# A decoder on one core: spread keys written by four GpSimd instructions, attention values copied by ScalarE

## The chip, the core and the metric

The kernel runs on one core of a Trainium2 chip. The core has five engines that run their own instruction queues and meet only at semaphores: TensorE (PE, matmuls, and PEld for its weight loads), VectorE (DVE), ScalarE (ACT), GpSimd (POOL) and SyncE (SP, here only DMA issues). They share the on-chip memory SBUF; TensorE writes its results to PSUM, which VectorE and ScalarE read. The metric is the time of one execution of the whole program in microseconds of the device.

## What is computed

The reference is a decoder of four layers with twelve steps on a hidden state of 64 x 64 x 128 floats (64 sequences of 64 tokens, width 128), each step added to the state. Three of its six attentions have 16 heads of width 8 over the tokens of one sequence, and keys of their own; two take keys and values from a second input, the context. The change touches the attentions of layers 1 to 3. Cut to what matters (`_layernorm` is a plain normalisation):

```
def _L1_attn_ref(x, Wqkv, bqkv, Wout, bout):              # phase a1
    q, k, v = split(x @ Wqkv + bqkv)                      # 16 heads of 8
    attn = softmax(q k^T / sqrt(8)); return (attn v) @ Wout + bout

def _L2_xattn_ref(query, key, value, wq, bq, wk, bk, wv, bv, wo, bo):   # phase x2
    q, k, v = query wq^T + bq, key wk^T + bk, value wv^T + bv
    attn = softmax(q k^T / sqrt(8)); return (attn v) wo^T + bo

def _L3_attn_ref(x, Wq, bq, Wk, bk, Wv, bv, Wo, bo, gamma, beta, rel_bias):  # phase a3
    xn = layernorm(x) * gamma + beta
    attn = q k^T * scale + rel; masked causally; softmax
    return (attn v) @ Wo.T + bo                           # v = xn @ Wv.T + bv

def _L3_xattn_ref(query, key, value, wq, wk, wv, bq, bk, bv):           # phase x3
    q, k, v = grouped_linear(...)                         # each with its bias
    src_max = maximum(max(score), 0)
    attn = exp(score - src_max) / (sum + exp(-src_max))   # restricted softmax
    return attn v                                         # no output projection
...
x = x + _L3_attn_ref(_layernorm(x), ...)
x = x + _L3_xattn_ref(_layernorm(x), ctx_1024, ctx_1024, ...)
```

## The kernel before

The program is a row of twelve phases, each closed by a barrier of all engines: a0, w0, f0, a1, x1, f1, a2, x2, f2, a3, x3, f3. The state `k.x` stays in SBUF all the time as 32 tiles of 128 tokens (two sequences each); eight groups of four tiles (`NG` = 8, `GT` = 4) go through each phase.

Function `attention` (L263) writes five of them: a0, a1, x2, a3 and x3. It writes one queue for each engine by hand, as Python loops over the 32 tiles i, with g the group and t = 0 to 3 the tile in it. Nothing is reordered later: the order of an engine is the order of these lines, and semaphores are the only ties between engines.

For each tile: TensorE `score(i+1)` (L847) makes scores of all 16 heads in one PSUM tile `S` of 128x1024; it works with *spread keys* `kbd`, in which each head has its own copy of the keys, multiplied by a mask `mask8` that keeps the 8 rows of that head. VectorE adds the relative bias where there is one (`add_bias`, L553, a3 only), takes the highest (L560, or L636 in a3), in x3 raises it to zero (a tensor_scalar, L647), and subtracts it into `e` (`shift`, L563). ScalarE takes the exponential in two halves (`exps`, L733). TensorE turns `e` into `TP` (`turn`, L858), ScalarE copies `TP` into `pT` in two halves (L738), TensorE weighs the values `vx` with it into `AV` (`weigh`, L871), and VectorE divides by the sums (`take_sums` and `take_values`, L534 and L548). All are staggered: while tile i is turned and weighed, tile i+1 is shifted and made exponential, and VectorE takes the values of tile i-1.

Between those steps, once in a group, stand the steps `early(g, t)` and `late(g, t)` of each engine:

- Values: `take_v(n, other)` of VectorE (L488 on) brings the projected values, from `PJ` (PSUM) or for kv="ctx" from `vin` (SBUF), into `vx`, where each head pair of the two sequences has its place. It is four instructions of 64x256 (L494), which also add the bias row `vb`; two stand before `shift` of t = 0 and two behind it. `v_ready` releases `weigh` and, in a1 and a3, the use of `PJ` by `turn_att` (L825) at t = 1.
- Keys: ScalarE writes heads 4 to 7 of `kbd` (`spread_keys`, L716, one instruction each: two at t = 0, one at t = 1, one at t = 2), GpSimd writes heads 0 to 3 (`spread_half`, L401) in one instruction of 128x2048. GpSimd waits for the keys (`kT_ready`, L708, at t = 3 for the group after the next, or the load of the context's keys) and for the last scores that read this half of `kbd`.
- Layernorm: VectorE takes statistics (t = 1) and gathers them (t = 2), GpSimd raises them to -0.5 (`norm_root`, L393), VectorE makes `nmr` from mean and root (`shift_mean`, L468, a scalar_tensor_tensor of 128x4, at t = 3), ScalarE normalises (L679, two tiles at t = 0 and two at t = 1), TensorE turns (L798, t = 2).
- Output: TensorE turns the attention output (L825) and projects it (L831), VectorE adds it to the state (`update`, L526), and GpSimd has by then added the output bias `ob` to the state (`bias_x`, L408). In x3 there is no output projection: `update` is L521, at t = 0.

The order of GpSimd in the loop is `bias_x(g)`, `norm_root(g + 3)`, `spread_half(g + 2)`. In the startup VectorE runs `whole_norm` of groups 0 and 1, then `take_v(0)`, in a3 the bias table `bt`, then `whole_norm(2)`; ScalarE works off groups 0 and 1, in a3 with a copy of the table's first product between them (`u`, L775), which TensorE multiplies (L918) before it turns group 1.

Function `warping` (L944, phase w0) also projects the context for the later phases, into DRAM: `project_memory` (L1255 on) and `stage_memory`, five products for each group, named in `jobs`. They run while VectorE works through a chain of small steps.

## Time and profile before

| what | us |
| --- | --- |
| median of 3 runs | 2355.95 (2353.13 to 2364.38) |
| the profiled execution, its own time | 2360.56 |
| its span in the trace | 2358.8 |
| phase a1 (L263 with tag a1), from its first to its last work | 707 to 889 |
| phase x2 | 1428 to 1593 |
| phase a3 | 1671 to 1885 |
| phase x3 | 1885 to 2065 |

Over the span TensorE is busy 76%, VectorE 57%, ScalarE 47%, GpSimd 31%; but phases differ, so each is read alone. The views used below are the timeline (instructions of one engine in order of time: start in us, duration in us, engine, line, operation, tile written and tiles read, shapes, count where several in a row are merged, and in brackets the idle time ahead of it and who ended it), the groups of instructions of a stretch (line, engine, operation, shapes, count, then busy us and mean ns of one, then idle time ahead and its releasers), and the windows (length of the stretch, busy us of PE, PEld, DVE, ACT and POOL with their counts, the granted clock of TensorE as a share of full speed, DMA share and GB/s). Durations of merged rows overlap by their tails: two copies of 0.58 follow each other at a distance of 0.49 and read 1.07 together.

### The profile page before, as it was taken

How to read it: one execution, taken by the hardware profiler on the slowest of the kernel's cores; microseconds unless marked ns; L12 is line 12 of the kernel's file. 1: busy time of each engine (PE TensorE's matmuls, PEld its weight loads, DVE VectorE, ACT ScalarE, POOL GpSimd, SP SyncE). 2: the span in 40 equal slices, each digit the busy share in tenths (PEclk: the TensorE clock that was granted, in tenths of full speed). 3: DMA queues.
4: the chain of work that ended last, by engine and by line, in shares of the span. 5: the costliest groups of instructions: out<-in, count | busy, mean ns of one | idle time of the engine just before them, and what ended most of it. 6: DMA issues, size and time to landing. Idle time of an engine off the chain costs nothing. (4 is left out here: it accounts for less than half of the span.)

```text
span 2358.8 us, 39307 instructions
## 1 busy us (share of the span) xinstructions
PE 1786.9 (76%) x14513; PEld 1229.5 (52%) x14513; DVE 1350.3 (57%) x3525; ACT 1103.6 (47%) x2265; POOL 730.6 (31%) x617
## 2 busy tenths in 40 slices
PE   3887562899987986778994886888788778851994
PEld 1554441545544664555994553655455535551774
DVE  2888578512235764554343467974399789851223
ACT  3676440333345766633442345763366566610441
POOL 1223201270463221155453003221222132156453
PEclk9888785699997998879997787999798878855997
DMA  4111272136615001112674001000000010012224
GB/s 152 82 83 83 86 246 58 28 98 165 177 48 213 33 2 55 29 38 99 213 236 154 1 1 36 29 10 10 3 2 2 2 45 24 6 40 69 64 80 137
DMA packets 143729, 173.18 MB, mean 73 GB/s; under 512 B 20913, under 2 KB 118897, under 8 KB 142609
## 3 DMA queue, kind: packets, MB, share of 16 engines
q1 hardware_dynamic: 123956, 129.09, 17.4%
q0 software_dynamic: 13248, 28.21, 3.5%
q10 hardware_dynamic: 6336, 13.37, 1.5%
q8 instruction: 118, 1.93, 0.3%
q14 instruction: 71, 0.58, 0.1%
HBM read 126.84 MB, written 79.05 MB: 87 GB/s over the span
## 5 line engine op out<-in xcount | busy, mean ns | idle before, releaser
L2770 POOL DMA_INDIRECT f_back<-f_ys,f_row x158 | 151.2, 957 | 173.7 <-DVE f_ys L2931 144.4
L871 PE MATMUL a_AV<-a_vx,a_pT 128*64 128x18 f32 (+1 forms) x3072 | 115.0, 223 | 42.3 <-DVE a_att L548 16.3
L2763 POOL DMA_INDIRECT f_slots<-f_pay,f_slot x128 | 124.5, 972 | 66.0 <-issue 38.2
L871 PEld LDWEIGHTS a_AV<-a_vx,a_pT 128*64 128x64 f32 x3072 | 105.9, 146 | 71.1 <-issue 36.7
L733 ACT ACTIVATE a_e<-a_e 128x512 f32<-128x512 f32 x192 | 110.2, 622 | 67.6 <-DVE a_e L563 67.6
L858 PE MATMUL a_TP<-ident,a_e 128*128 128x128 f32 x768 | 110.2, 288 | 19.0 <-ACT a_e L733 18.4
L738 ACT COPY a_pT<-a_TP 128x512 f32<-128x512 f32 x192 | 103.7, 588 | 41.9 <-PE a_TP L858 41.7
L858 PEld LDWEIGHTS a_TP<-ident,a_e 128*128 128x128 f32 x768 | 91.4, 148 | 57.5 <-ACT a_e L733 45.8
L847 PE MATMUL a_S<-a_kbd,a_qT 64*64 64x512 f32 x768 | 118.3, 693 | 0.9 <-issue 0.6
L563 DVE TENSOR_TENSOR a_e<-a_S,a_mx 128x1024 f32<-128x1024 f32 x96 | 117.3, 1221 | 2.9
L560 DVE TENSOR_REDUCE a_mx<-a_S 128x16 f32<-128x1024 f32 x66 | 80.8, 1224 | 42.8 <-PE a_S L847 41.6
L2997 ACT ACTIVATE f_h<-f_H,f_wt 128x256 f32<-128x256 f32 x156 | 67.0, 474 | 81.5 <-PE f_H L3093 81.5
L2997 ACT ACTIVATE f_h<-f_H,f_b 128x512 f32<-128x512 f32 (+1 forms) x96 | 57.7, 616 | 83.3 <-PE f_H L3093 83.3
L858 PEld LDWEIGHTS x_TP<-ident,x_e 128*128 128x128 f32 x512 | 62.5, 153 | 61.3 <-ACT x_e L733 51.7
L871 PE MATMUL x_AV<-x_vx,x_pT 128*64 128x18 f32 x2048 | 77.1, 219 | 21.8 <-ACT x_pT L738 15.0
L858 PE MATMUL x_TP<-ident,x_e 128*128 128x128 f32 x512 | 78.6, 300 | 17.8 <-ACT x_e L733 17.5
L560 DVE TENSOR_REDUCE x_mx<-x_S 128x16 f32<-128x1024 f32 x64 | 78.1, 1220 | 22.5 <-PE x_S L847 22.1
L871 PEld LDWEIGHTS x_AV<-x_vx,x_pT 128*64 128x64 f32 x2048 | 71.9, 148 | 35.4 <-issue 25.7
L1653 ACT ACTIVATE f_h<-f_H,f_b 128x512 f32<-128x512 f32 x64 | 44.0, 687 | 94.0 <-PE f_H L1761 93.9
L393 POOL TENSOR_TENSOR a_rstd<-a_var,neghalf 128x4 f32<-128x4 f32 x24 | 24.3, 1015 | 204.9 <-DVE a_var L464 120.9
L716 ACT ACTIVATE a_kbd<-a_kT,a_mask 128x512 f32<-128x512 f32 x128 | 85.6, 723 | 0.4
L401 POOL TENSOR_TENSOR a_kbd<-a_kT,a_mask 128x2048 f32<-128x2048 f32 x16 | 57.6, 3600 | 85.8 <-ACT a_kT L708 85.8
(481 smaller groups left out, 4611.8 us busy)
## 6 DMA issues: line engine op xcount, KB each, us to landing
f_wt<-in_f_ew SPq DMA_DIRECT2D x39, 584.0 KB
f_slots<-in_blank SPq DMA_DIRECT2D x1, 18576.0 KB
f_wt<-in_f_leaf SPq DMA_DIRECT2D x94, 98.0 KB, 2.0
f_pay<-f_back SPq DMA_DIRECT2D x8, 1024.0 KB, 5.6
f_xs<-f_slots SPq DMA_DIRECT2D x47, 144.0 KB
memory_x_k<-w_stage ACTq DMA_DIRECT2D x24, 256.0 KB, 3.1
f_slots<-in_blank SPq DMA_DIRECT2D x1, 5760.0 KB
f_xs<-leaf_slots SPq DMA_DIRECT2D x22, 256.0 KB, 3.6
```

What stands on the lines that cost most here:

```text
L401: pool.tensor_tensor(kbd[:, n % 2, :, 0:4, :], bc(keys(n).rearrange("p (b j) -> p b j", j=SL), 2, shape), mask8[:, 0:4].unsqueeze(1).unsqu ...
L560: return v.tensor_reduce(mx[:, i % 2, :], unit(i), AX.X, ALU.max)
L563: v.tensor_tensor(e[:, i % 2, :, :], unit(i), bc(mx[:, i % 2, :], 2, [P, NH, SL]), ALU.subtract).then_inc(shifted.sem, 1)
L716: last = act.activation(kbd[:, n % 2, :, h, :], keys(n).rearrange("p (b j) -> p b j", j=SL), ACT.Copy, scale=mask8[:, h:h + 1])
L733: act.activation(eh, eh, ACT.Exp).then_inc(weights.sem, 1)
L738: act.copy(pT[:, 4 * n:4 * n + 4, :], TP[:, n, :].rearrange("p (a b) -> p a b", a=4)).then_inc(pT_half.sem, 1)
L847: last = pe.matmul(S[64 * c:64 * c + 64, i % 2, r, :], qT[rows, g % 2, SL * b:SL * b + SL], kbd[rows, g % 2, b, :, :], start=True, stop=True)
L858: last = pe.transpose(TP[:, half, P * n:P * n + P], ev[:, 4 * half + n, :], k.ident[:, :])
L871: last = pe.matmul(AV[64 * c:64 * c + 64, 2 * hp * W1:2 * (hp + 1) * W1], pT[:, hp, 64 * c:64 * c + 64], vx[:, g % 2, t, c, 2 * hp:2 * hp ...
L2763: pool.indirect_dma_start(out=slots[:, :], out_offset=bass.IndirectOffsetOnAxis(ap=slot[:, c, t:t + 1], axis=0), in_=pay[:, c, t, :], in_o ...
L2770: pool.indirect_dma_start(out=back[:, :], out_offset=bass.IndirectOffsetOnAxis(ap=row[:, i % RR, t:t + 1], axis=0), in_=ys[:, i % RY, t, : ...
L2997: act.activation(h[:, i % 2, c, 0:P * n], hid(i, c, n), ACT.Gelu_apprx_tanh, bias=weights(i)[2][:, c:c + 1])\
```

## The change

Four things change.

1. `spread_half` writes heads 0 to 3 in four GpSimd instructions, each for two of the eight sequences of the group (128x512), in a1, x2, a3 and x3. The semaphore is raised by the last one.
2. In a3 and x3 (`act_moves=True`) VectorE no longer has `take_v`; ScalarE does it, as four copies of 64x256 without bias, behind the two copies of `pT` at t = 0, and for group 0 in the startup. Of the keys, ScalarE then spreads head 4 at t = 0, heads 5 and 6 at t = 1 and head 7 at t = 2.
3. The values' bias of a3 goes to the output: since the weights of a row sum to one, bias times output matrix is added to the output bias once, by one TensorE product at the start of the phase and one VectorE add into `obr`, which `bias_x` then adds.
4. The values' bias of x3 goes into the context's projection in w0: four further products with one row each (a column of ones times the bias row), for each group.

```
@@ spread_half
-                    shape = [P, 2 * GT, 4, SL]
-                    pool.tensor_tensor(kbd[:, n % 2, :, 0:4, :], bc(keys(n).rearrange("p (b j) -> p b j", j=SL), 2, shape),
-                                       mask8[:, 0:4].unsqueeze(1).unsqueeze(3).to_broadcast(shape), ALU.mult).then_inc(kbd_pool.sem, 1)
+                    shape = [P, 2, 4, SL]
+                    kv = keys(n).rearrange("p (b j) -> p b j", j=SL)
+                    for b in range(0, 2 * GT, 2):
+                        last = pool.tensor_tensor(kbd[:, n % 2, b:b + 2, 0:4, :], bc(kv[:, b:b + 2, :], 2, shape),
+                                                  mask8[:, 0:4].unsqueeze(1).unsqueeze(3).to_broadcast(shape), ALU.mult)
+                    last.then_inc(kbd_pool.sem, 1)
@@ bias_x
+                    if g == 0 and obr is not None:
+                        pool.wait_ge(ob_ready.sem, 1)
+                    added = obr[:, :] if obr is not None else k.row(ob)
@@ VectorE: early, late
-                    if g + 1 < NG:
+                    if g + 1 < NG and not act_moves:
                         take_v(g + 1, False)
...
@@ VectorE: startup
+            if not act_moves:
+                v.wait_ge(setup_done.sem, 2)
+                take_v(0, False)
+                take_v(0, True)
+            elif obr is not None:
+                v.wait_ge(ob_product.sem, 1)
+                v.tensor_tensor(obr[:, :], AV[:, 0:P], k.row(ob), ALU.add).then_inc(ob_ready.sem, 1)
@@ ScalarE
+            def take_v(n):
+                if cross:
+                    act.wait_ge(kv_in[n % 2].sem, kv_in[n % 2].after(n // 2))
+                else:
+                    act.wait_ge(v_product.sem, v_product.after(n))
+                if n >= 2:
+                    act.wait_ge(values.sem, values.after(GT * (n - 2) + GT - 1))
+                for half in range(2):
+                    for seq in range(2):
...
+                        last = act.copy(vx[rows, n % 2, :, seq, half:NH:2, 0:width], src)
+                last.then_inc(v_ready.sem, 1)
             def late(g, t):
+                if act_moves and t == 0 and g + 1 < NG:
+                    take_v(g + 1)
                 if t < 3 and g and g + 1 < NG:
-                    spread_keys(g + 1, ((0, 1, 2), (3, 4, 5), (6, 7))[t] if diff else ((4, 5), (6,), (7,))[t])
+                    spread_keys(g + 1, ((0, 1, 2), (3, 4, 5), (6, 7))[t] if diff else
+                                ((4,), (5, 6), (7,))[t] if act_moves else ((4, 5), (6,), (7,))[t])
@@ ScalarE: startup, behind spread_keys(0) and take_q(0)
+            if act_moves:
+                act.wait_ge(setup_done.sem, 2)
+                take_v(0)
@@ TensorE
+            if obr is not None:
+                pe.matmul(AV[:, 0:P], k.col(vb).to_broadcast([P, P]), k.mat(o), start=True, stop=True).then_inc(ob_product.sem, 1)
@@ project_memory in w0
+                            if bias is not None:
+                                last = pe.matmul(banks[n][:, tok], ones[0:1, 0:1].to_broadcast([1, P]), k.row(bias)[0:1, :], start=False, stop=True)
```

How the queues stand before and after at the places that matter. First ScalarE in a3, in the first group that spreads keys, from the last tile of the group before to the second tile of this one, before:

```order
L738 COPY a_pT<-a_TP 128x512 x2
L716 ACTIVATE a_kbd<-a_kT,a_mask 128x8x64 x2
L679 ACTIVATE a_xn<-x,a_nmr,a_rstd 128x128 x2
L733 ACTIVATE a_e<-a_e 128x512 x2
L679 ACTIVATE a_xn<-x,a_nmr,a_rstd 128x128 x2
L725 COPY a_attT<-a_PJ 128x512
L738 COPY a_pT<-a_TP 128x512 x2
L716 ACTIVATE a_kbd<-a_kT,a_mask 128x8x64
L733 ACTIVATE a_e<-a_e 128x512 x2
```

The same stretch after:

```order
L768 COPY a_pT<-a_TP 128x512 x2
L747 COPY a_vx<-a_PJ 64x4x8x8 x4
L729 ACTIVATE a_kbd<-a_kT,a_mask 128x8x64
L692 ACTIVATE a_xn<-x,a_nmr,a_rstd 128x128 x2
L763 ACTIVATE a_e<-a_e 128x512 x2
L692 ACTIVATE a_xn<-x,a_nmr,a_rstd 128x128 x2
L755 COPY a_attT<-a_PJ 128x512
L768 COPY a_pT<-a_TP 128x512 x2
L729 ACTIVATE a_kbd<-a_kT,a_mask 128x8x64 x2
L763 ACTIVATE a_e<-a_e 128x512 x2
```

Four copies now stand ahead of the exponentials of the second tile, one spread of keys has moved behind them. In x3 it is the same without `a_attT`.

Then ScalarE in the startup of a3, where `a_u` is the first product of the bias table, before:

```order
L708 ACTIVATE a_kT<-a_PJ,cols 128x512
L716 ACTIVATE a_kbd<-a_kT,a_mask 128x8x64 x4
L775 COPY a_u<-a_S 32x1024
L687 ACTIVATE a_xT<-a_PJ,cols 128x512
L697 ACTIVATE a_qT<-a_PJ,cols 128x512
```

and after:

```order
L721 ACTIVATE a_kT<-a_PJ,cols 128x512
L729 ACTIVATE a_kbd<-a_kT,a_mask 128x8x64 x4
L747 COPY a_vx<-a_PJ 64x4x8x8 x4
L811 COPY a_u<-a_S 32x1024
L700 ACTIVATE a_xT<-a_PJ,cols 128x512
L710 ACTIVATE a_qT<-a_PJ,cols 128x512
```

The copies of the values stand between the keys and the copy that the bias table waits for.

## Rows read from the trace of the kernel before

**Rows 1.** Windows: one of a1, one of a3, two of x3.
```profile
780.00:800.00 20.00, 18.34 (x225) 12.12 (x224) 15.63 (x34) 15.47 (x31) 5.86 (x3) 1.00 0.01 2
...
1722.00:1845.00 123.00, 104.12 (x1160) 70.46 (x1161) 116.90 (x175) 80.88 (x148) 31.38 (x16) 0.89 0.01 2
...
1926.00:1946.00 20.00, 15.76 (x218) 9.96 (x216) 19.21 (x41) 15.51 (x33) 4.88 (x3) 1.00 0.09 27
...
1966.00:1986.00 20.00, 17.44 (x173) 11.52 (x171) 16.94 (x39) 12.69 (x27) 3.27 (x3) 0.66 0.01 2
```

**Rows 2.** Timeline of a3 from 1748 us: GpSimd, then VectorE.
```profile
1748.90 3.60 POOL L401 TENSOR_TENSOR a_kbd<-a_kT,a_mask 128x2048 f32<-128x2048 f32 x1 [2.57 <-ACT a_kT L708]
1752.46 1.27 POOL L408 TENSOR_TENSOR x<-x,rows 128x512 f32<-128x512 f32 x1
...
1749.01 3.51 DVE L468 SCALAR_TENSOR_TENSOR a_nmr<-a_mv,a_rstd 128x4 f32<-128x4 f32 x1
```

**Rows 3.** Timeline of x3 from 1944 us: GpSimd, then VectorE.
```profile
1944.30 3.60 POOL L401 TENSOR_TENSOR x_kbd<-x_kT,x_mask 128x2048 f32<-128x2048 f32 x1
...
1945.10 2.83 DVE L647 TENSOR_SCALAR x_mx<-x_mx 128x16 f32<-128x16 f32 x1
```

**Rows 4.** Two lines over the span: count, then ns minimum/median/maximum, first and last start.
```profile
L468 DVE SCALAR_TENSOR_TENSOR a_nmr<-a_mv,a_rstd x24: 149/161/3510, 28.8 to 1819.2; 128x4 f32<-128x4 f32 x24
...
L647 DVE TENSOR_SCALAR x_mx<-x_mx x30: 174/175/2836, 1916.1 to 2059.1; 128x16 f32<-128x16 f32 x30
```

**Rows 5.** Groups of instructions of a3, 1745 to 1843 us.
```profile
L733 ACT ACTIVATE a_e<-a_e 128x512 f32<-128x512 f32 x34 | 19.5, 622 | 18.0 <-DVE a_e L563 18.0
```

**Rows 6.** Groups of instructions of x3, 1926 to 2006 us.
```profile
L494 DVE TENSOR_TENSOR x_vx<-x_vin,rows 64x256 f32<-64x256 f32 x16 | 6.7, 418 | 0.2
```

**Rows 7.** Timeline of GpSimd: its spreads in a3 and x3, first and last of each.
```profile
1726.20 3.60 POOL L401 TENSOR_TENSOR a_kbd<-a_kT,a_mask 128x2048 f32<-128x2048 f32 x1 [2.56 <-ACT a_kT L708]
...
1842.87 3.60 POOL L401 TENSOR_TENSOR a_kbd<-a_kT,a_mask 128x2048 f32<-128x2048 f32 x1 [18.91 <-ACT a_kT L708]
...
1924.61 3.60 POOL L401 TENSOR_TENSOR x_kbd<-x_kT,x_mask 128x2048 f32<-128x2048 f32 x1
...
2005.00 3.60 POOL L401 TENSOR_TENSOR x_kbd<-x_kT,x_mask 128x2048 f32<-128x2048 f32 x1
```

**Rows 8.** Timeline of ScalarE in a3 from 1751 us: the start of a group.
```profile
1751.72 1.07 ACT L738 COPY a_pT<-a_TP 128x512 f32<-128x512 f32 x2 [1.45 <-PE a_TP L858]
1752.68 1.34 ACT L716 ACTIVATE a_kbd<-a_kT,a_mask 128x512 f32<-128x512 f32 x2
1753.91 0.87 ACT L679 ACTIVATE a_xn<-x,a_nmr,a_rstd 128x128 f32<-128x128 f32 x2
```

**Rows 9.** Timeline of the startups of x3 (VectorE, ScalarE) and x2 (VectorE).
```profile
1894.22 3.55 DVE L468 SCALAR_TENSOR_TENSOR x_nmr<-x_mv,x_rstd 128x4 f32<-128x4 f32 x1 [1.12 <-POOL x_rstd L393]
...
1897.81 1.65 ACT L679 ACTIVATE x_xn<-x,x_nmr,x_rstd 128x128 f32<-128x128 f32 x4 [2.04 <-DVE x_nmr L468]
...
1436.44 3.55 DVE L468 SCALAR_TENSOR_TENSOR x_nmr<-x_mv,x_rstd 128x4 f32<-128x4 f32 x1 [1.12 <-POOL x_rstd L393]
```

**Rows 10.** Timeline of VectorE inside x2, from 1502 us.
```profile
1502.13 1.34 DVE L468 SCALAR_TENSOR_TENSOR x_nmr<-x_mv,x_rstd 128x4 f32<-128x4 f32 x1
...
1504.20 1.23 DVE L560 TENSOR_REDUCE x_mx<-x_S 128x16 f32<-128x1024 f32 x1 [0.44 <-PE x_S L847]
```

**Rows 11.** Timeline of the startup of a3: ScalarE, then TensorE.
```profile
1689.54 1.00 ACT L775 COPY a_u<-a_S 32x1024 f32<-32x1024 f32 x1 [0.20 <-PE a_S L910]
...
1689.43 2.08 PE L815 MATMUL a_PJ<-mats,a_xT 128*128 128x128 f32 x8
1691.44 3.78 PE L918 MATMUL a_S<-a_u,a_mt 32*128 32x512 f32 x4
```

**Rows 12.** Timeline of TensorE in w0: its first work behind the context's projection.
```profile
386.76 0.64 PE L1286 MATMUL w_TX<-ident,w_C 64*64 64x32 f32 x8 [50.60 <-DVE w_found L1096]
```

**Rows 13.** Timeline of TensorE in x3: transposes behind a wait.
```profile
2040.97 1.97 PE L858 MATMUL x_TP<-ident,x_e 128*128 128x128 f32 x8 [1.24 <-ACT x_e L733]
```

More of the change, by code:

```diff
@@ L37 @@
 COLS = ["a0_g", "a0_b", "a1_bq", "a1_bk", "x1_nw", "a2_ga", "a2_be", "a2_bq", "x2_bq", "x2_bk",
-        "a3_bq", "a3_bk", "a3_ga", "a3_be", "x3_bq", "x3_bk"]
+        "a3_bq", "a3_bk", "a3_ga", "a3_be", "x3_bq", "x3_bk", "a1_bv", "x2_bv", "a3_bv"]
 ROWS = ["a1_bv", "a1_bo", "x1_gb", "x1_nw", "a2_bq", "a2_bk", "a2_bv", "a2_bqa", "a2_bka",
@@ L263, in attention @@
 def attention(nc, k, d, tag, q, kk, vv, o=None, kv="self", width=8, qb=None, kb=None, vb=None,
-              ob=None, affine=None, bias=False, restricted=False, diff=None, fill=None):
+              ob=None, affine=None, bias=False, restricted=False, diff=None, fill=None, act_moves=False):
     ph = Phase(nc, tag)
@@ L292, in attention @@
     attT = ph.sb("attT", [P, GT, P]) if o is not None else None
+    obr = ph.sb("obr", [P, P]) if act_moves and o is not None else None
+    ob_product, ob_ready = ph.counter("ob_product"), ph.counter("ob_ready")
     S = ph.ps("S", [P, 2, 2, 512])
@@ L407, in bias_x @@
                     pool.wait_ge(xn_ready.sem, xn_ready.after(g))
-                    pool.tensor_tensor(xg, xg, bc(k.row(ob), 1, [P, GT, P]), ALU.add).then_inc(x_biased.sem, 1)
+                    if g == 0 and obr is not None:
+                        pool.wait_ge(ob_ready.sem, 1)
+                    added = obr[:, :] if obr is not None else k.row(ob)
+                    pool.tensor_tensor(xg, xg, bc(added, 1, [P, GT, P]), ALU.add).then_inc(x_biased.sem, 1)
             def square(g):
@@ L595, in late @@
                 if t == 0:
-                    if g + 1 < NG:
+                    if g + 1 < NG and not act_moves:
                         take_v(g + 1, True)
@@ L718, in spread_keys @@
                     last.then_inc(kbd_ready.sem, 1)
+            def take_v(n):
[7 more added lines that the diff above has]
+                    for seq in range(2):
+                        src_rows, rows = slice(64 * seq, 64 * seq + 64), slice(64 * half, 64 * half + 64)
+                        src = flat(vin[src_rows, n % 2, :, :]) if cross else PJ[src_rows, :]
+                        src = src.rearrange("p (t h w) -> p t h w", t=GT, w=width)
+                        if not diff:
+                            src = src[:, :, half:NH:2, :]
+                        last = act.copy(vx[rows, n % 2, :, seq, half:NH:2, 0:width], src)
+                last.then_inc(v_ready.sem, 1)
             def take_att(g):
@@ L1187, in stage_memory @@
                     dst = stage[:, g % 2, n, :]
-                    if bias is None:
+                    if bias is None or not turned:
                         act.copy(dst, banks[n]).then_inc(staged.sem, 1)
@@ L1267, in project_memory @@
                             tok = slice(P * t, P * t + P)
-                            last = pe.matmul(banks[n][:, tok], cT[:, g % 2, tok], k.mat(name), start=True, stop=True)
+                            last = pe.matmul(banks[n][:, tok], cT[:, g % 2, tok], k.mat(name), start=True, stop=bias is None)
+                            if bias is not None:
+                                last = pe.matmul(banks[n][:, tok], ones[0:1, 0:1].to_broadcast([1, P]), k.row(bias)[0:1, :], start=False, stop=True)
                     last.then_inc(projected.sem, 1)
@@ L3201, in lay_out @@
             "x2_bq": i["L2_xattn_bq"], "x2_bk": i["L2_xattn_bk"], "a3_bq": i["L3_attn_bq"], "a3_bk": i["L3_attn_bk"],
-            "a3_ga": i["L3_attn_gamma"], "a3_be": i["L3_attn_beta"], "x3_bq": i["L3_xattn_bq"], "x3_bk": i["L3_xattn_bk"]}
+            "a3_ga": i["L3_attn_gamma"], "a3_be": i["L3_attn_beta"], "x3_bq": i["L3_xattn_bq"], "x3_bk": i["L3_xattn_bk"],
+            "a1_bv": bqkv[:, 2].reshape(P), "x2_bv": i["L2_xattn_bv"], "a3_bv": i["L3_attn_bv"]}
     d["cols"] = np.stack([cols[n] for n in COLS], axis=1)
```

11 lines of the change are left out of this document (4 added, 7 removed).

## The prediction

> **What bounds the kernel now.** Phases are closed by barriers, so what a phase gains comes off the total. I read the windows first [rows 1]. In a1 TensorE is busy 18.3 of 20 us and its clock is granted in full: matmuls and their hand-overs set the pace. In a3 VectorE is busy 116.9 of 123 us, in x3 19.2 of 20 where the clock is full. There it is VectorE, and ScalarE says the same: in a3 its exponentials waited 18.0 us in a stretch of 98, all for VectorE's subtraction [rows 5].
>
> Part of this busy time is no work. In a3 the tiny scalar_tensor_tensor L468 takes 3.51 us and ends at 1752.52, when GpSimd's spread that began 0.11 us before it ends at 1752.50 [rows 2]; its siblings take 0.15 [rows 4], and each of groups 0 to 4 of a3 has one like this. In x3 the tensor_scalar L647 takes 2.83 instead of 0.17 [rows 3, 4] and ends at 1947.93, the spread at 1947.90; it is 2.66 lost in each of the same groups. So these two kinds of VectorE instruction, all operands in SBUF, wait until a running GpSimd instruction ends. Reductions and subtractions from PSUM beside it keep their 1.2 us. And the hand-over happens between two GpSimd instructions that stand back to back: L408 starts at 1752.46 with nothing ahead of it missing, and L468 still ends at 1752.52 [rows 2].
>
> The pace is read off the spreads [rows 7]: six in a3 from 1726.20 to 1842.87, five steps, 23.3 us for a group; five in x3 from 1924.61 to 2005.00, four steps, 20.1 (three of 19.7, one of 21.3, the one whose window shows a clock of 0.66).
>
> **Part 1, four GpSimd instructions.** A piece costs between 0.90 (3.60 / 4) and 1.27, the price of another GpSimd tensor_tensor of 128x512, L408 [rows 2]. I take 1.0, between them and nearer the first, whose operands are these. The whole then ends 0.4 later (bounds 0 and 1.5); the keys are read a group later, `bias_x` behind it is read by `update` some five us later, so this is hidden; it would take over 4 us more to show. VectorE now waits for one piece at most. In a3 L468 comes 0.11 behind the start, so it waits about 0.9 instead of 3.36: 2.5 less, in five groups (0 to 4). In x3 the tensor_scalar falls late in the first piece and L468 behind it into the third: about 0.3 + 0.6 instead of 2.66, so 1.8 less, again in five groups and a bit in the sixth. In x2 one such wait is 1.34 long, but the reduction behind it then waits 0.44 for TensorE [rows 10], which had been busy: nothing is gained. In a1 the two do not meet. In the startups of x2 and x3 the L468 of group 1 is held for 3.55 and ScalarE waits for it 2.04 [rows 9]; without it ScalarE normalises earlier, then meets the query product that starts at the same time: I count 1.5 in x2 and 1.2 in x3 (bounds 0 and 2.0).
>
> **Part 2, the copies.** VectorE loses four instructions of 0.42 [rows 6], with their gaps 1.75 a group, seven times in each phase. ScalarE gains four copies that no row shows. From its pairs [rows 8] a spread of 512 elements takes 0.63 to the next, a normalisation of 128 takes 0.38, a plain copy of 512 takes 0.48: so 0.24 for 384 elements, and a plain copy of 256 would take 0.32. Bounds are 0.25 and 0.48. I take 0.33, 1.3 for four. The Trainium skill, Perfetto Trace Analysis, section Optimizing Scalar/DVE Operations, gives ScalarE about 51 ns of fixed cost on PSUM and 93 on SBUF, and advises larger operations on a saturated engine, which speaks against cutting work into four. Taking its 51 ns with the 1.2 GHz of the skill's first page, an estimate is 0.26 a copy, 1.1 for four, and the sum would gain about 3 us more; no row here shows it.
>
> **Is ScalarE then in the way?** At t = 0 it had 1.34 + 0.87 of spreads and normalisations ahead of the exponentials [rows 8], about 2.0 by distances; now 1.3 + 0.63 + 0.77 = 2.7, and 0.63 more at t = 1. Per group VectorE alone would need 23.3 - 1.75 - 2.5 = 19.1 in a3 and 19.7 - 1.75 - 1.8 = 16.2 in x3. I followed one group through the three queues, with what the timeline of these stretches gives as distances at full clock: scores 1.0, bias 1.1, highest 1.25, subtract 1.15 (a3 3.7 from scores to ready), half an exponential 0.6, transposes 1.0, copy 0.7, weighing 1.05, projections 1.0 each. In a3 the scores of successive tiles start at 0, 4.4, 11.0, 15.1, 20.1; in x3 at 0, 3.4, 9.0, 13.0, 17.4. The long second step is that of ScalarE: the copies delay the second tile's exponentials, and TensorE waits about 1.2 (a3) and 1.5 (x3) for them. So the pace becomes 20.1 in a3 and 17.4 in x3, 1.0 and 1.2 above VectorE's own.
>
> **Startup of a3.** Here the copies cost. The value product starts at 1689.43 and takes 2.08, the table's copy was done by 1690.54 and TensorE multiplied it from 1691.44 [rows 11]. Now ScalarE waits for the product (1691.5), copies values (1692.8) and the table (1693.9), and TensorE, which turns group 1 only behind that product, is 2.5 late.
>
> **Parts 3 and 4.** One product and one add of 128x128 in a3's startup stand where both engines idle: nothing. The 32 products in w0 follow work after which TensorE idles 50.6 us [rows 12]; each could take 1.5 before anyone waited. Nothing.
>
> **The sum.** a3: five steps of 3.2 = 16.0; first and last groups 1.0; startup -2.5; together 14.5. x3: four steps of 2.7 = 10.8; behind 2005.00 one wait of each kind and two value copies, 2.7 + 2.3 + 3.5 less 1.5 left over, of which half, since TensorE sets the end there: 3.5; the first group 1.5; startup 1.2; together 17. x2: 1.5. Total 33. The profiled execution took 2360.56, so 2327.6; the runs' median stands 0.2% under that, 2355.95, and 33 from it gives 2323. I take **2324**.
>
> **Rivals.**
>
> *TensorE's clock decides (more ScalarE than counted).* Copies at their bound of 0.48 add 0.6 a group. TensorE's waits then pass 1.8, and in x3 a wait of 1.24 was once followed by 1.97 for eight transposes [rows 13], twice the 1.0 above: the level of 1.2 GHz. Such a stretch costs 1.6 of a group now (21.3 against 19.7), with VectorE holding the pace; if it comes in half the groups at 2 us, 12 of the 33 go. With the copies 18 or so go: 2339. For it: more rests on TensorE now. Against it: a1 keeps the full clock with waits under 1 us.
>
> *No hand-over between pieces.* VectorE waits for all four, 0.4 longer than now. Then a3 goes at 21.9 and x3 at 18.4, 1.4 and 1.3 a group for seven groups, less 2.5: 2356 - 17 = 2340. The hand-over of [rows 2] speaks against it. The skill's page SBUF — State Buffer, section Who interferes with whom, has the shared port pair locked for a whole instruction, whoever comes first; by it the trace agrees with one piece of waiting, and it does not say who is served between pieces.
>
> *VectorE's bound alone.* If the copies hide (0.25 each), a3 runs at 19.2 and x3 at 16.3: 1 us more for 12 groups, 2311.
>
> *Slower: half clock all through.* If TensorE waits over 2 us behind the copies in each group, it may stay at 1.2 GHz for most of it. In x3 its 13.7 us of a group [rows 1] double to 27, in a3 17 to 34. It decides once half clock holds for over a quarter of a3's group (3.2 us lost) and a fifth of x3's. At 40% of each, a group of a3 takes 25 and one of x3 22: 2356 + 8 + 9 = 2373. The mean 0.89 in both phases [rows 1], with waits of 2.1, says that this is far.
>
> *Nothing shows.* If x3 and a3 were bound by TensorE anyway, 2355; the 18.0 us of ScalarE waiting for VectorE [rows 5] speak against it.
>
> **How the numbers follow.** Forecast 0.60 (2314 to 2333), clock 0.16, no hand-over 0.06, VectorE's bound 0.11, slower 0.04, nothing 0.03. A measurement of this kernel can tell 0.5%, about 12 us, from no change. Faster needs under 2344: the forecast, its upper rival, and most of the clock's and hand-over's: 0.88. Same 0.08, slower 0.04. The range leaves out the last two rivals and the tails of the others: 2308 to 2342.
>
> **What would show it.** L468 in a3 and L647 in x3 never over 1.3 us. Spreads of a3 about 20 apart, of x3 about 17.5, each in four pieces of 1.0. ScalarE's copies at 0.33 each. The wait of TensorE behind ScalarE's exponentials largest at the second tile of a group. The table's product in a3's startup 2.5 later than now. Wrong would be: pieces that hold VectorE for 4 us, copies of 0.5, or a granted clock under 0.85 in a3 and x3.

## The result, and the profile after

The changed kernel takes 2341.77 us (median of 11 runs, 2338.58 to 2350.8), the kernel before in the same comparison 2360.02 (11 runs): a ratio of 0.9933, interval 0.9915 to 0.995. It is faster by 18 us. The forecast was 33. The profiled execution has a span of 2340.2.

The table takes the phases out of the two traces. A phase begins with GpSimd's first memset of its vx; a3 ends where x3 begins, x3 with VectorE's last update of x (the next phase starts 0.9 us later; the figures for x3 in the expectations include that). "Step" is the distance of two spreads of GpSimd in the steady groups.

| phase | before | after | gain | forecast |
| --- | --- | --- | --- | --- |
| a3, us | 214.4 | 203.4 | 11.0 | 14.5 |
| a3, step | 23.3 | 20.56 | 2.7 | 3.2 |
| x3, us | 180.0 | 177.4 | 2.6 | 17 |
| x3, step | 20.1 | 20.46 | -0.4 | 2.7 |
| all else | 1964.4 | 1959.4 | 5.0 | 1.5 |

GpSimd first: the timeline of its spreads in the changed kernel, which answers [rows 7]. The first two are consecutive ones of a3, the last two of x3.
```profile
1743.90 4.04 POOL L406 TENSOR_TENSOR a_kbd<-a_kT,a_mask 128x512 f32<-128x512 f32 x4 [2.57 <-ACT a_kT L721]
1764.47 4.04 POOL L406 TENSOR_TENSOR a_kbd<-a_kT,a_mask 128x512 f32<-128x512 f32 x4 [2.57 <-ACT a_kT L721]
...
1949.41 4.04 POOL L406 TENSOR_TENSOR x_kbd<-x_kT,x_mask 128x512 f32<-128x512 f32 x4
1969.89 4.04 POOL L406 TENSOR_TENSOR x_kbd<-x_kT,x_mask 128x512 f32<-128x512 f32 x4
```
Four pieces take 4.04, 1.01 each as forecast. And VectorE's two kinds of stalled instruction, from the timeline beside the spreads at 1764.47 (a3) and 1949.41 (x3), where [rows 2, 3] had 3.51 and 2.83:
```profile
1764.58 0.95 DVE L477 SCALAR_TENSOR_TENSOR a_nmr<-a_mv,a_rstd 128x4 f32<-128x4 f32 x1
...
1951.26 0.22 DVE L660 TENSOR_SCALAR x_mx<-x_mx 128x16 f32<-128x16 f32 x1
1952.66 0.81 DVE L477 SCALAR_TENSOR_TENSOR x_nmr<-x_mv,x_rstd 128x4 f32<-128x4 f32 x1
```
So the stall is gone in both phases: VectorE is served between two pieces. But x3's step did not follow. The reason stands on TensorE. Its timeline over one group of x3:
```profile
1956.87 1.09 PE L883 MATMUL x_S<-x_kbd,x_qT 64*64 64x512 f32 x8
1959.98 1.64 PE L894 MATMUL x_TP<-ident,x_e 128*128 128x128 f32 x8 [2.02 <-ACT x_e L763]
1961.83 1.90 PE L907 MATMUL x_AV<-x_vx,x_pT 128*64 128x18 f32 x32 [0.21 <-ACT x_pT L768]
1963.66 1.98 PE L883 MATMUL x_S<-x_kbd,x_qT 64*64 64x512 f32 x8
...
1966.48 1.46 PE L894 MATMUL x_TP<-ident,x_e 128*128 128x128 f32 x8
```
It waits 2.02 us for ScalarE's exponentials of the group's second tile, and from there to about 1967.5 the same matmuls take twice their 1.09 and 1.11: the level of 1.2 GHz. Every steady group of x3 looks like this. In a3 the wait is split in two and the level stays at 2.4 GHz:
```profile
1771.93 1.18 PE L894 MATMUL a_TP<-ident,a_e 128*128 128x128 f32 x8 [1.19 <-ACT a_e L763]
1773.83 1.16 PE L867 MATMUL a_PJ<-mats,a_attT 128*128 128x128 f32 x8 [0.72 <-ACT a_attT L755]
```
The windows say it for both (a3, then x3; length, busy us of PE, PEld, DVE, ACT, POOL, granted clock, DMA share, GB/s), beside 0.89 and 1.00/0.66 in [rows 1]:
```profile
1744.00:1826.00 82.00, 70.77 (x880) 46.89 (x878) 72.91 (x116) 66.22 (x128) 24.03 (x23) 1.00 0.01 2
1908.00:1990.00 82.00, 68.55 (x796) 45.06 (x800) 62.97 (x141) 62.97 (x137) 20.22 (x21) 0.83 0.07 21
```
What TensorE waits for is this piece of ScalarE's timeline, the same group: the four new copies stand ahead of the exponentials (L763) and take 1.73, not 1.3. The copies' line below it gives minimum, median and maximum in ns.
```profile
1956.06 1.73 ACT L747 COPY x_vx<-x_vin 64x256 f32<-64x256 f32 x4
1957.81 0.72 ACT L729 ACTIVATE x_kbd<-x_kT,x_mask 128x512 f32<-128x512 f32 x1
1958.44 0.86 ACT L692 ACTIVATE x_xn<-x,x_nmr,x_rstd 128x128 f32<-128x128 f32 x2
...
L747 ACT COPY a_vx<-a_PJ x32: 366/388/407, 1686.0 to 1831.1; 64x256 f32<-64x256 f32 x32
L747 ACT COPY x_vx<-x_vin x32: 393/423/446, 1882.9 to 2018.8; 64x256 f32<-64x256 f32 x32
```

**Theory A**: in x3 the copies on ScalarE make TensorE wait 2.0 us, which drops its clock, and these two together eat what the split gave. **Theory B**: something else, ScalarE's own sum of work or GpSimd's, sets x3's step at 20.4, whatever the clock.

### The profile page after: what moved, and what is told of

It is laid out like the page before. It is cut to its first block and busy times, and to the rows that moved or that the text cites. A ratio compares the mean times of both kernels' runs of the same rounds, so it can differ in the third digit from the quotient of the medians.

```text
span 2340.2 us, 39550 instructions
## 1 busy us (share of the span) xinstructions
PE 1792.2 (77%) x14579; PEld 1234.2 (53%) x14579; DVE 1295.4 (55%) x3462; ACT 1129.0 (48%) x2329; POOL 745.6 (32%) x713
## 3 DMA queue, kind: packets, MB, share of 16 engines
q1 hardware_dynamic: 123956, 129.09, 17.9%
## 5 line engine op out<-in xcount | busy, mean ns | idle before, releaser
L763 ACT ACTIVATE a_e<-a_e 128x512 f32<-128x512 f32 x192 | 110.1, 623 | 50.1 <-DVE a_e L572 50.1
L907 PE MATMUL x_AV<-x_vx,x_pT 128*64 128x18 f32 x2048 | 77.8, 219 | 21.3 <-ACT x_pT L768 15.0
L406 POOL TENSOR_TENSOR a_kbd<-a_kT,a_mask 128x512 f32<-128x512 f32 x64 | 64.6, 1041 | 81.7 <-ACT a_kT L721 81.7
```

The lines of the kernel that those rows point to most:

```text
L763: act.activation(eh, eh, ACT.Exp).then_inc(weights.sem, 1)
L907: last = pe.matmul(AV[64 * c:64 * c + 64, 2 * hp * W1:2 * (hp + 1) * W1], pT[:, hp, 64 * c:64 * c + 64], vx[:, g % 2, t, c, 2 * hp:2 * hp ...
```

## The experiments

The experiments ran on other chips, where the kernel before takes about 2490 and the changed one about 2470. The difference lies ahead of a3, most of it in f0, whose weights are transferred there at half the rate (last section). The changed kernel was profiled there twice more: a3 took 208.1 and 203.3 where its first profile has 203.4, x3 176.4 and 174.1 for 177.4. So phases can be compared across chips to within such differences, whole times only by their ratio to the runs of before beside them. The kernel before has one profile, on the first chip. Lengths are those of the table above, each from one profile.

| kernel | a3 | step | x3 | step | ratio to before (interval) |
| --- | --- | --- | --- | --- | --- |
| before | 214.4 | 23.3 | 180.0 | 20.1 | 1 |
| changed kernel | 203.4 | 20.56 | 177.4 | 20.46 | 0.9933 (0.9915 to 0.995) |
| split alone | 198.0 | 20.23 | 162.9 | 17.80 | 0.9885 (0.9832 to 0.9938) |
| moves alone | 207.9 | 21.5 | 181.0 | 21.3 | 0.9976 (0.9953 to 1.0) |
| moves in a3 alone, split | 203.3 | 20.56 | 162.2 | 17.80 | 0.9878 (0.9823 to 0.9933) |
| changed, two products more | 203.3 | 20.55 | 164.1 | 18.0 | 0.9888 (0.9833 to 0.9943) |
| changed, x3's copies in idle spots | 207.8 | 20.6 / 23.4 | 159.4 | 17.4 | 0.9884 (0.9849 to 0.9919) |
| changed, two of x3's copies | 203.3 | 20.56 | 157.7 | 17.3 | 0.99 (0.9864 to 0.9937) |
| changed, three of x3's copies | 203.4 | 20.56 | 166.6 | 17.6 to 19.5 | 0.9887 (0.9848 to 0.9926) |
| changed, u first | 200.6 | 20.56 | 173.9 | 20.4 | 0.996 (0.9938 to 0.9982) |
| changed, exponentials ahead | 208.0 | 20.6 to 23.4 | 169.9 | 17.9 to 20.4 | 0.997 (0.9948 to 0.9991) |
| new order in both | 191.3 | 19.03 | 162.4 | 17.4 | 0.9825 (0.9789 to 0.9862) |
| split, x3's moves in idle spots | 199.8 | 20.23 | 160.5 | 17.4 | 0.9877 (0.9849 to 0.9905) |

### The two parts apart

The split alone is the kernel before with this edit and no other:
```
-                    pool.tensor_tensor(kbd[:, n % 2, :, 0:4, :], ...)
+                    for b in range(0, 2 * GT, 2):
+                        last = pool.tensor_tensor(kbd[:, n % 2, b:b + 2, 0:4, :], ...)
```


> The kernel before with GpSimd's spread in four instructions and nothing else: VectorE still copies the values. What is in question: the share of each part in the changed kernel's 18 us, and why x3 gained 2.6 us where 17 were forecast. Theory A (in x3 TensorE waits 2.0 us behind ScalarE's four copies and is then granted half the clock): without the copies on ScalarE the wait is not there, only VectorE's stall goes, so x3's spreads start 20.1 - 1.8 = 18.3 us apart and x3 takes about 170 us, less than the changed kernel's 178.3; a3's spreads start 23.3 - 2.5 = 20.8 apart (a3 about 201); the whole 2355.95 - 12 - 10 - 1 = about 2333, under the changed kernel. Theory B (ScalarE's or TensorE's own work sets x3's pace): x3's spreads stay at 20 or more apart, x3 about 179, the whole 2343. Both expect no VectorE wait over 1.3 us at the line of nmr (scalar_tensor_tensor) anywhere.

Measured: a3 198.0 and x3 162.9, in the two phases 33.5 us less than before and **20 us less than the changed kernel**. VectorE has no stall over one piece; for the whole span the line of nmr reads
```profile
L471 DVE SCALAR_TENSOR_TENSOR a_nmr<-a_mv,a_rstd x24: 151/164/945, 28.6 to 1935.0; 128x4 f32<-128x4 f32 x24
```
TensorE's largest waits in the steady groups of x3 are 1.06 to 1.26, and its clock is full in a3 and in x3 but for one group: behind a wait of 1.06 it fell for a short time, and that group took 18.8 (from the turning at 2095.30 to the one at 2114.10). Two rows of TensorE, then a window of a3 and two of x3:
```profile
2095.30 1.18 PE L861 MATMUL x_TP<-ident,x_e 128*128 128x128 f32 x8 [1.06 <-ACT x_e L736]
...
2098.65 1.98 PE L850 MATMUL x_S<-x_kbd,x_qT 64*64 64x512 f32 x8
...
1874.00:1954.00 80.00, 70.61 (x880) 46.74 (x878) 78.42 (x132) 60.22 (x113) 24.16 (x23) 1.00 0.01 2
2034.00:2087.00 53.00, 43.42 (x595) 27.27 (x594) 50.67 (x118) 41.65 (x90) 14.47 (x15) 1.00 0.09 25
2087.00:2105.00 18.00, 15.07 (x198) 9.80 (x198) 17.07 (x40) 14.35 (x31) 5.21 (x6) 0.91 0.07 23
```
x3's usual step of 19.7 becomes 17.8: the 1.9 of a stall, as sized. a3's falls by 3.1, more than the 2.5 of its stall, since the half clock of before (0.89 in [rows 1]) goes as well. The changed kernel's gain is thus all the split's, and theory A holds in its first half: without the copies on ScalarE the wait of 2.0 is gone, and with it the half clock in every group.

The other part alone, the changed kernel with the spread in one instruction again (the edit above undone):

> The changed kernel with GpSimd's spread back in one instruction: the moves of copies and bias alone. Both theories: VectorE stalls behind GpSimd again (3.4 us once a group in a3, some 2.8 in x3). Theory A: x3 pays both, since the copies' wait at TensorE and the stall come in different tiles: spreads 20.4 to 22 apart, x3 180 to 190; a3 23.3 - 1.75 = 21.5 apart, a3 phase 214.4 - 8 + 2.5 = 209; the whole about 2350 to 2358. Theory B: x3 exactly as in the changed kernel (20.4 apart, 178), since the stall was never the bound there; the whole about 2348.

Measured: ratio 0.9976, a3 207.9, x3 181.0, which is 1.0 us more than before. Both costs come in each group of x3, at different tiles, as theory A said. The rows show TensorE's wait at 2075.92 and, 12 us later, VectorE's stall behind the whole spread.
```profile
2075.92 1.56 PE L891 MATMUL x_TP<-ident,x_e 128*128 128x128 f32 x8 [2.01 <-ACT x_e L760]
2077.77 1.90 PE L904 MATMUL x_AV<-x_vx,x_pT 128*64 128x18 f32 x32 [0.29 <-ACT x_pT L765]
...
2087.72 1.74 DVE L657 TENSOR_SCALAR x_mx<-x_mx 128x16 f32<-128x16 f32 x1
```

The moves in a3 alone: x3 is called as in the kernel before, with its bias (`vb="x3_bv"`), and w0's job for x3_v has none.

> The changed kernel, but x3 keeps its copies and the bias on VectorE (the memory projection of w0 has no bias product again); a3 as changed, four GpSimd instructions in both. Theory A: x3 no longer has the 2.0 us wait and the half clock behind it: spreads 18.3 apart, x3 about 170 instead of 178.3; the whole 2341.8 - 8 = about 2334. Theory B: x3 as it was, 20.4 apart, or slower by the copies on VectorE (1.75 us a group): 2342 to 2350.

Measured: x3 162.2 at 17.80 a step, shorter even than theory A's 170, a3 203.3. So the moves, beside the split, cost 15 us in x3 and 5.3 in a3 (12 and 3.5 in the profiles of the five rounds below).

### Is it the clock?

The next kernel does more work and takes no wait away. In x3, ahead of the turning that waits:
```
+                if t == 1 and cross and act_moves and g + 1 < NG:
+                    pe.wait_ge(q_ready.sem, q_ready.after(g + 1))
+                    for _ in range(2):
+                        pe.matmul(PJ[:, :], k.mat(q), xT[:, :, :], start=True, stop=True)
```


> The changed kernel, and in x3 TensorE makes two products more (128 x 512 into the free bank PJ, nobody reads them) at the second tile of each group, ahead of the turning that waits for ScalarE's exponentials. At the full clock such a product takes some 0.95 us, so that they fill the wait of 2.0. It is more work and takes away no wait of ScalarE's. Theory A: the clock stays granted through the group, spreads 17.4 to 18 apart, x3 about 160 to 164, the whole about 2325. Theory B (ScalarE's or GpSimd's own work sets the pace): spreads stay 20.4 apart or more, the whole 2342 or slower.

Measured: steps of 18.0, x3 164.1, 13 us less than the changed kernel's 177.4 (10 less than its shortest x3, 174.1), with two products more in every group. The timeline of TensorE at the same place:
```profile
2083.11 1.09 PE L883 MATMUL x_S<-x_kbd,x_qT 64*64 64x512 f32 x8
2084.13 1.98 PE L917 MATMUL x_PJ<-x_xT,mats 128*128 128x512 f32 x4
2086.22 1.18 PE L894 MATMUL x_TP<-ident,x_e 128*128 128x128 f32 x8
2088.07 1.11 PE L907 MATMUL x_AV<-x_vx,x_pT 128*64 128x18 f32 x32 [0.67 <-ACT x_pT L768]
```
TensorE starts its turning no earlier behind the scores (3.1 us, as in the changed kernel), but what follows stays at full speed, and so does the whole steady stretch of x3, where the changed kernel had 0.83:
```profile
2035.00:2125.00 90.00, 80.31 (x1016) 49.42 (x1013) 80.65 (x171) 76.78 (x168) 25.04 (x25) 1.00 0.09 25
```
Theory B, under which extra work can't help, is out. 2.5 us of a step come back: **the clock, not the wait itself, is the price**.

Then the same work in other places: two copies ahead of the first pair's turned tile, two ahead of xT.
```
             def early(g, t):
+                if act_moves and cross and t in (0, 2) and g + 1 < NG:
+                    take_v(g + 1, (t // 2,))
```


> The changed kernel; in x3 ScalarE makes two of the four copies ahead of the turned tile of a group's first pair and two ahead of xT of its third, where it stood idle 1.07 and 2.11 us, instead of all four behind the first pair's turned tile. The same work for every engine. Theory A (wait behind the copies, then half the clock): TensorE's wait for the exponentials falls from 2.02 by about 1.7, the clock stays, spreads 17.4 to 18 apart, x3 160 to 164, the whole about 2325. Theory B (ScalarE's own work is the bound): 20.4 apart, the whole 2342.

Measured: 17.4 a step, the very step that was forecast, x3 159.4. The wait at the second tile has become small:
```profile
2090.46 1.18 PE L898 MATMUL x_TP<-ident,x_e 128*128 128x128 f32 x8 [0.41 <-ACT x_e L765]
```

### Waits of 1.3 and 1.7 us

Two kernels leave copies out, in the changed kernel's place: one makes two of the four (half the heads get no new values in x3), one makes three.

> The changed kernel, where ScalarE makes only two of x3's four copies, so that the values of half the heads are left out in x3. In the same place. Theory A: TensorE's wait for the exponentials is 2.0 - 0.87 = 1.15 us, as in a3 where the clock stays; spreads about 17.5 apart, x3 160, the whole about 2325: nearly three microseconds a group for 0.87 of work. Theory B (ScalarE's own work): spreads 20.4 - 0.9 = 19.5 apart, x3 about 172, the whole 2335.

> The changed kernel with three of x3's four ScalarE copies, so that part of the values of the heads 0, 2, ... (of each tile's first sequence) is left out in x3. Three copies of 0.42 are 1.27 us, the very 1.3 at which the prediction put four. If the size of the copies was the only wrong term, the wait for the exponentials is 2.02 - 0.43 = 1.6, the clock stays at its full level and the spreads start 17.3 to 17.5 apart, x3 about 158 to 160, as forecast. If the sum also took a wait for harmless that is not, the granted clock falls in some or all groups behind 1.6 us too: spreads 18 to 20 apart, x3 165 to 172.

Measured: with two copies the wait is 1.31, the clock is full in every steady group, 17.3 a step (0.9 us of work less gave 3.1 us a step). With three the wait is 1.73 and the steps are 17.59, 19.46, 18.24, 19.46. Two groups of it that follow each other, with the same wait and another clock:
```profile
2060.57 1.97 PE L896 MATMUL x_TP<-ident,x_e 128*128 128x128 f32 x8 [1.73 <-ACT x_e L765]
...
2080.54 1.18 PE L896 MATMUL x_TP<-ident,x_e 128*128 128x128 f32 x8 [1.73 <-ACT x_e L765]
```
Three of the five steady groups lose the clock. Three copies of 0.42 are the 1.3 that the prediction counted for four. So two things were wrong, not one: the copies' size, and what comes of 1.3 us of copies, which is a wait of 1.73 and not 1.5, and half clock behind it in some groups. Whether a wait of 1.5 would leave the clock alone, no run shows. The length of the last wait alone does not decide it: the clock stayed behind 1.31 here, and in another kernel (the exponentials ahead, below) behind one of 1.92, but fell behind 1.06 in one group of the split alone and behind 1.24 in [rows 13].

### a3: the startup, and the edge

For the startup, `act.copy(u...)` stands ahead of `take_v(0)`, nothing else:

> The changed kernel, where ScalarE at the start of a3 takes the table u before it copies the first values. If the 2.74 us that TensorE waited for u are on the path, a3 is 2.0 to 2.7 shorter (203.4 to about 201) and the whole 2339.3; if the first values or their weights end last in their place, nothing changes.

Measured: a3 200.6, 2.8 shorter, and the product of the table follows the values' without a wait. Here is the changed kernel, then this one:
```profile
1688.65 3.78 PE L956 MATMUL a_S<-a_u,a_mt 32*128 32x512 f32 x4 [2.74 <-ACT a_u L811]
```
```profile
1807.92 2.08 PE L851 MATMUL a_PJ<-mats,a_xT 128*128 128x128 f32 x8
1809.92 3.78 PE L956 MATMUL a_S<-a_u,a_mt 32*128 32x512 f32 x4
```
The forecast of this cost (2.5) was right, and it was avoidable. The whole time does not show the gain: the ratio is 0.996, and the ten runs lie between 2465 and 2487.

In the kernel with x3's copies in idle spots, whose a3 is unchanged, a3 took 207.8. So the changed kernel ran again:

> The changed kernel as it is, beside the two that follow. What is in question is whether a3 under it is steady: in its profile every group took 20.5, while in two of six kernels with the same a3 some groups took 22 to 23.4 at a granted clock of 0.85. If a3 stands at the edge of losing the clock, a3 lies between 203 and 211 us from run to run and the runs spread over some 8 us or more; if those groups belong to the other kernels' edits, a3 is 203.4 again. x3 177 us under both, 20.4 a group. Against before a ratio of about 0.993.

Measured: a3 208.1, with steps of 23.58 and 23.42 among those of 20.56; the ratio to before 0.99 (0.9881 to 0.9918). One such group of this run:
```profile
1851.97 1.18 PE L894 MATMUL a_TP<-ident,a_e 128*128 128x128 f32 x8 [1.20 <-ACT a_e L763]
1853.87 2.07 PE L867 MATMUL a_PJ<-mats,a_attT 128*128 128x128 f32 x8 [0.72 <-ACT a_attT L755]
...
1857.70 1.98 PE L883 MATMUL a_S<-a_kbd,a_qT 64*64 64x512 f32 x8
```
The waits are those of the first profile, 1.2 and 0.72; the clock falls behind them here and not there. Of nine profiles with this steady a3, two have such groups (two each, 2.9 us a group). The changed kernel's a3 stands at that edge too.

### A better order

First, a failure. Besides the two reorderings above, the exponentials of the second pair were put ahead of the spread and the two xn tiles that stood before them, and these behind:
```
                 take_turned(i)
+                if act_moves and t == 0:
+                    if not cross and g + 1 < NG:
+                        take_v(g + 1)
+                    exps(i + 1)
                 late(g, t)
```


> The changed kernel with three reorderings and the same work: x3's copies in ScalarE's idle spots (two ahead of the first pair's turned tile, two ahead of xT), u before the first values in a3, and in both attentions the exponentials of a group's second pair ahead of the spread heads and xn that stood before them. Theory A: neither a3 nor x3 has a TensorE wait over 0.7 us at the second pair; a3 spreads 19.5 to 20 apart (a3 about 197), x3 17 to 17.5 (x3 about 160); the whole about 2317 to 2322. Theory B: a3 20.5, x3 20.4 as in the changed kernel, the whole 2339.

Measured: theory A's times were missed, a3 208.0 and x3 169.9, the ratio 0.997. The wait for the exponentials did go, but one spread and four xn tiles now stood between them and the copies that TensorE wants next, and it waited as long for those (a3, then x3):
```profile
1900.36 1.33 PE L873 MATMUL a_PJ<-mats,a_attT 128*128 128x128 f32 x8 [2.10 <-ACT a_attT L757]
1901.62 1.90 PE L913 MATMUL a_AV<-a_vx,a_pT 128*64 128x18 f32 x32
...
2071.70 1.79 PE L913 MATMUL x_AV<-x_vx,x_pT 128*64 128x18 f32 x32 [2.05 <-ACT x_pT L770]
```
Behind these waits TensorE is at half clock again (1.90 and 1.79 for the weighing's 1.11): its order failed by the very mechanism of theory A.

Second, an order in which nothing that can wait stands ahead of what TensorE waits for. x3 as in the kernel with the idle spots, u first, and in a3:
```
+                if act_moves and not cross:      # early
+                    if t == 0 and g and g + 1 < NG:
+                        spread_keys(g + 1, (4, 5))
+                    if t == 1 and g:
+                        take_att(g - 1)
...
+                if act_moves and not cross:      # late
+                    if t == 0 and g + 1 < NG:
+                        take_v(g + 1)
+                    if t == 1 and g + 2 < NG:
+                        normalize(g + 2, range(GT))
+                    if t in (1, 2) and g and g + 1 < NG:
+                        spread_keys(g + 1, (t + 5,))
```


> The changed kernel with the same work in another order on ScalarE. x3: two copies ahead of the first pair's turned tile and two ahead of xT. a3: u before the first values; spread heads 4 and 5 ahead of the first pair's turned tile (where ScalarE waited 1.44 for TensorE), then the copies and at once the second pair's exponentials; attT and pT of the second pair, and all four xn tiles behind them. If the waits of 1.19 and 0.72 us for ScalarE are what holds a3 at 20.5, they go (neither over 0.4), the spreads start 18.7 to 19.3 apart and a3 takes 188 to 193 (changed kernel 203.4); x3 159 to 160; together some 30 less than the changed kernel, a ratio to before of about 0.981. If TensorE's own matmuls or VectorE are the bound of a3, it stays at 20.2 to 20.5, about 200, and only x3 gains: ratio about 0.985. If the order only moves the wait to attT or pT, as in the kernel with the exponentials ahead, a3 is 205 or more.

Measured: a3 191.3 at 19.03 a step, x3 162.4; ratio 0.9825. TensorE no longer waits for the second pair at all, and the spreads lie where ScalarE stood idle (timeline of TensorE, then of ScalarE, then a window):
```profile
1874.31 1.16 PE L916 MATMUL a_TP<-ident,a_e 128*128 128x128 f32 x8
1875.42 1.16 PE L889 MATMUL a_PJ<-mats,a_attT 128*128 128x128 f32 x8
...
1869.48 1.32 ACT L729 ACTIVATE a_kbd<-a_kT,a_mask 128x512 f32<-128x512 f32 x2
1871.02 1.07 ACT L770 COPY a_pT<-a_TP 128x512 f32<-128x512 f32 x2 [0.21 <-PE a_TP L916]
1871.98 1.59 ACT L748 COPY a_vx<-a_PJ 64x256 f32<-64x256 f32 x4
1873.60 1.15 ACT L765 ACTIVATE a_e<-a_e 128x512 f32<-128x512 f32 x2
...
1855.00:1935.00 80.00, 75.60 (x936) 49.80 (x938) 77.08 (x129) 69.51 (x138) 25.14 (x24) 1.00 0.01 2
```
In this window of 80 us VectorE is busy 77.08 and TensorE 75.60, and the step of 19.03 is the 19.1 that the prediction had for VectorE alone. So the copies that VectorE lost seem to count only now; which of the two engines sets this step was not tried.

The other candidate keeps a3 as before with the split, and moves in x3 alone:

> The kernel before with the spread in four instructions, and in x3 alone the copies on ScalarE, in its idle spots; a3 keeps copies and bias on VectorE. By the parts measured apart: a3 198.0, x3 159.4, together 357.4 against 394.4 of before and 380.8 of the changed kernel: a ratio to before of 0.985, and 20 us or more under the changed kernel. If the moves pay once they are placed well, this is behind the kernel with the new order in both; if they pay nowhere but in x3, it is ahead of it.

Measured: 199.8 and 160.5, ratio 0.9877. The ratios of this kernel and of the new order overlap in their intervals, but a3 is 8.5 us longer here and x3 1.9 shorter. So in a3 too the moves pay, once placed.

Last, side by side on one chip in five rounds, what the phases had said from profiles of several:

> The changed kernel beside the split alone and the new order on one chip. From the phases: a3 and x3 together 381 to 385 us. Ratio to before 0.990 to 0.993.

> The kernel before with the spread in four instructions alone. If the moves of copies and bias cost 16 to 20 us in a3 and x3, as the phases of the profiles say, this is 15 to 20 us faster than the changed kernel on the same chip (a ratio to before of 0.985 to 0.987; a3 198, x3 163). If the phases mislead, or the moves give it back elsewhere (the bias product in w0, f3), the two are within 5 us.

> The changed kernel's work in the new order of ScalarE. a3 191, x3 159 to 162: 25 to 30 us under the changed kernel and 5 to 10 under the split alone, a ratio to before of 0.980 to 0.983.

| kernel | median us | ratio to before (interval) | a3 | x3 |
| --- | --- | --- | --- | --- |
| before | 2489.14 | 1 | | |
| changed kernel | 2470.73 | 0.9927 (0.9901 to 0.9953) | 203.3 | 174.1 |
| split alone | 2457.75 | 0.9882 (0.9854 to 0.9909) | 199.8 | 162.5 |
| new order | 2447.01 | 0.9827 (0.9803 to 0.9851) | 193.1 | 160.6 |

No run of one of these kernels falls among those of another. The split alone is 13 us under the changed kernel, a little less than the 15 expected (15.1 in the two phases of these profiles); the new order is 24 under it and 42 under before, the 25 to 30 not quite reached.

## Why the prediction was wrong

**The four pieces: right.** 1.01 each (taken 1.0), VectorE's waits 0.8 for 0.9 in a3 (0.95 less the bare instruction's 0.16), in x3 0.05 to 0.1 and 0.65 for 0.3 and 0.6. The hand-over between two GpSimd instructions, read from [rows 2], was what the change needed. The Trainium skill, SBUF — State Buffer, section Who interferes with whom, has the shared ports locked for a whole instruction; the trace agrees, with 3.5 us behind one instruction of 3.6 and 0.95 behind one of 1.01. Worth by itself 33.5 us in a3 and x3, where the part's own terms (2.5 and 1.8 a group, the startup) come to some 23. The prediction did not count that the half clock behind the stalls would go with them (0.89 before, 1.00 in a3 and 0.98 in x3's steady stretch of the split alone).

**The copies: right on VectorE, mis-sized on ScalarE.** 0.39 from PSUM and 0.42 from SBUF, taken 0.33, inside the bounds of 0.25 and 0.48. Four are 1.59 and 1.73, taken 1.3. The scaling from rows of full width [rows 8] does not hold for these copies of 64 partitions into a strided tile; which of the two makes them dearer was not tried.

**"Is ScalarE then in the way?": the step that failed.** It found the wait, its place and its cause, and gave it 1.5 in x3 and 1.2 in a3; it was 2.02 and 1.19. Then it reckoned every distance behind the wait "at full clock". That is where x3's gain went: with two extra products in the gap x3 takes 164.1, without them 177.4 (174.1 to 177.4 in three profiles), so 10 to 13 of the 14 us by which x3 fell short. The right size of the copies is not all of it: three copies, which take the 1.3 that it did count, lose the clock in three of five groups. The row that it had for this [rows 13], half clock behind 1.24, stood in the rival and not in the sum. And it did not ask what the stall that the change removes had done to TensorE: the trace of before has waits of 2.23 for the exponentials in three groups of x3, each with half clock behind it.
```profile
1969.71 1.97 PE L858 MATMUL x_TP<-ident,x_e 128*128 128x128 f32 x8 [2.23 <-ACT x_e L733]
...
1973.44 1.98 PE L847 MATMUL x_S<-x_kbd,x_qT 64*64 64x512 f32 x8
```
The change took this wait away and put one of 2.02 in its place.

**The rival "TensorE's clock decides" was the case.** It got 0.16. It had the mechanism, the place, and 2339 for a measured 2341.8, though its own terms, 18 off the 33, give 2341 from 2356. What it had wrong was the argument against itself, that a1 keeps its clock with waits under 1 us: the waits that it had to judge were longer. The rivals of no hand-over, of VectorE's bound and of no effect fell; that of half clock all through fell by size (0.83 in x3, a step of 20.5 and not 22). Two readings were off and decided nothing. The stall in x3, put at 2.66 in every group, was 1.9, 2.7, 2.7, 1.6 and 2.7. And the 13.7 us of TensorE's work in a group of x3 come out of the distances at full clock (4.0 + 4.0 + 4.2 + 1.5) and do not stand in [rows 1], which has 15.8 of 20.

**The startups.** In a3 the table's product came 2.74 later (taken 2.5), and avoidably so. In x3 the 1.2 did not come: the nmr instruction takes 0.99 for 3.55 [rows 9], but TensorE waits 2.81 for the first weights and is at 1.2 GHz until about 1905. The first and the last of those rows:
```profile
1892.79 1.97 PE L894 MATMUL x_TP<-ident,x_e 128*128 128x128 f32 x8 [2.81 <-ACT x_e L763]
...
1902.31 1.98 PE L883 MATMUL x_S<-x_kbd,x_qT 64*64 64x512 f32 x8
```
With the copies on VectorE (the split alone) the same wait of 2.83 is followed by half clock for 6 us. But in the changed kernel's profile of the five rounds it lasted some 8 and not 12, so this differs between executions of one kernel; what sets it was not tried.

**Outside a3 and x3** the span is 5.0 shorter, where 1.5 was counted for x2. There 0.7 came, and it is the split's: with the spread in one instruction again x2 takes 165.3, as before (165.2), and in most other runs 164.5. Phases whose code did not change differ between the two profiles by several us in both directions (f0 is 4.7 shorter, f1 5.0 longer); this remainder was not traced to a cause.

**The sum.** a3 11.0 for 14.5, x3 2.6 for 17, x2 and the rest 5 for 1.5. In a3 the step had one wait and there were two: the 0.72 for the turned attention output was not in it, and the pace is 20.56 for 20.1. The direction, the mechanism of the split and the range (2308 to 2342, just) held; the size did not.

## What to carry to other kernels

Follow a wait that you expect on TensorE one step further: give it two prices, with and without half clock behind it, and let the worse one into the sum if the trace has a single row of half clock behind a wait no longer than it. If the stall that you remove has such a wait of its own, ask whether the change puts another in its place. Work that is moved to an engine with idle time must go into that idle time: name the instruction ahead of which it is queued and who waits for that one. And where an engine stalls behind a long instruction of a port neighbour, cut that instruction first, alone, and measure before adding relief that may no longer be needed.
